# Experts of a group beside the two halves of the first attention of the next two groups

## The reference

```python
x = x + tanh(g_xattn[0]) * L0_xattn(layernorm(x), ctx)   # 16 heads of 16; q and k normed per head; the last
                                                         # 16 context rows have weights and a softmax of their own
x = x + tanh(g_ffn[0]) * L0_ffn(layernorm(x))            # router: top 4 of 16 experts of 64, and a shared expert
x = x + tanh(g_xattn[1]) * L1_xattn(layernorm(x), ctx)   # 16 query heads of 128, 8 key and value heads
x = x + tanh(g_ffn[1]) * L1_ffn(layernorm(x))            # weights looked up in a table of 16 values
```

## Time and profile before

| what | value |
|---|---|
| median of 3 runs | 504.74 us (504.55 to 507.48) |
| the profiled execution: own time | 506.47 us |
| the profiled execution: span | 504.5 us |
| mean granted TensorE clock, share of full | 0.904 |
| start to the first scores' end | 0 to 40.8 us |
| phase A from there | 40.8 to 163.1 us |
| phase B | 163.1 to 278.8 us |
| phases C and D | 278.8 to 504.5 us |

### The profile page before, as it was taken

One profiled execution on the slowest core, in us unless ns is written; L12 is line 12 of the kernel. 1 busy time (PEld: TensorE's weight loads), 2 busy tenths in 40 slices (PEclk: granted clock), 3 DMA queues, 4 the chain that ended last, 5 costly groups with the idle time before them and its releaser, 6 DMA issues.

```text
span 504.5 us, 8784 instructions
## 1 busy us (share of the span) xinstructions
PE 420.9 (83%) x3040; PEld 394.6 (78%) x3040; DVE 344.3 (68%) x754; ACT 204.9 (41%) x404; POOL 162.3 (32%) x195
## 2 busy tenths in 40 slices
PE   0546895958565999999999899999999999598896
PEld 0435774848465999999998899989988989597795
DVE  4776758486702657667675589889889979935542
ACT  2344535554311232333233366366366365222231
POOL 3014223131320121222313244463463564422232
PEclk9959695976855899999999999999999999988999
DMA  8102010010200002020200100100100100000000
GB/s 253 32 29 98 0 59 3 1 64 0 105 0 1 0 1 105 0 104 0 104 0 14 52 1 2 56 0 0 54 0 0 44 1 0 1 0 22 23 11 32
DMA packets 6633, 16.03 MB, mean 32 GB/s; under 512 B 1090, under 2 KB 4291, under 8 KB 6100
## 3 DMA queue, kind: packets, MB, share of 16 engines
q1 hardware_dynamic: 6612, 15.75, 9.3%
HBM read 14.70 MB, written 1.05 MB: 31 GB/s over the span
## 4 chain that ended last, share of the span: by engine, by line
PE 36%; issue 27%; DVE 15%; POOL 12%; ACT 7%; DMA 2%; POOLq 0%; DVEq 0%; ACTq 0%; SPq 0%
PE ps L290 19%; PE ps L485 5%; DVE work L1361 5%; POOL workr L1012 4%; PE ps L1091 4%; PE ps L475 2%; POOL workA L566 2%; ACT workA L510 1%; POOL wB_lo L572 1%; POOL rstd L255 1%; POOL work L1409 1%; POOL work L1419 1%; PE ps L360 1%; DVE shared_r L1323 1%; PE ps L1112 1%
## 5 line engine op out<-in xcount | busy, mean ns | idle before, releaser
L290 PE MATMUL ps<-wB_hi,workr 128*128 128x256 f32 (+1 forms) x224 | 52.7, 298 | 11.0 <-POOL workr L1574 10.2
L1419 POOL TENSOR_SCALAR work<-work,lut_step,lut 128x344 f32<-128x344 int32 (+1 forms) x60 | 41.7, 707 | 55.6 <-DVE work L1346 53.8
L290 PE MATMUL ps<-xT_hi,wB_hi 128*128 128x256 f32 x176 | 53.4, 303 | 0.0
L290 PE MATMUL ps<-xT_lo,wB_hi 128*128 128x256 f32 x176 | 51.6, 293 | 0.0
L290 PE MATMUL ps<-xT_hi,wB_lo 128*128 128x256 f32 x176 | 51.6, 293 | 0.0
L290 PEld LDWEIGHTS ps<-wB_hi,workr 128*128 128x128 f32 (+1 forms) x224 | 39.2, 192 | 13.2 <-issue 11.5
L290 PE MATMUL ps<-wN_hi,shared_r 128*128 128x256 f32 x256 | 48.0, 282 | 1.3 <-DVE x L1333 1.3
L1012 POOL TENSOR_TENSOR workr<-work,workr 128x256 fp32r<-128x256 f32 (+1 forms) x36 | 22.9, 637 | 74.1 <-ACT workr L895 74.1
L1361 DVE COPY_PREDICATED work<-work 128x1376 f32<-128x1376 int32 (+5 forms) x36 | 42.8, 1190 | 2.7 <-DVE work L1361 0.3
L290 PEld LDWEIGHTS ps<-wN_hi,shared_r 128*128 128x128 f32 x256 | 40.4, 188 | 1.5 <-DVE shared_r L1323 1.5
L290 PE MATMUL ps<-xT_hi,wM_hi 128*128 128x256 f32 x128 | 36.7, 287 | 3.9 <-ACT work L1187 2.4
(11 more groups left out here) (202 smaller groups left out, 1216.8 us busy)
## 6 DMA issues: line engine op xcount, KB each, us to landing
stage<-in_wC SPq DMA_DIRECT2D x4, 1280.0 KB, 5.4
stage<-in_wB SPq DMA_DIRECT2D x4, 768.0 KB, 4.3
stage<-in_idx SPq DMA_DIRECT2D x4, 536.0 KB, 3.4
stage<-in_wA SPq DMA_DIRECT2D x2, 512.0 KB, 5.5
out<-x SPq DMA_DIRECT2D x4, 256.0 KB, 2.2
x<-in_x SPq DMA_DIRECT2D x1, 768.0 KB, 7.1
ctx_T<-in_ctx_T SPq DMA_DIRECT2D x1, 512.0 KB, 7.4
ctx_n<-in_ctx_n SPq DMA_DIRECT2D x4, 128.0 KB, 2.2
```

Of the source, the lines that this page charges most:

```text
L290: last = nc.tensor.matmul(out, l, r, start=start and i == 0, stop=stop and i == 2)
L1419: nc.gpsimd.tensor_scalar(lev[:, j, 0:n], bits[:, 0, 0:n], lut_step[:, j:j + 1], lut[:, 2 * j:2 * j + 1], ALU.mult, ALU.add).then_inc(*C[" ...
```

## The change

Phases A and B become one. The new `pe_AB`, `act_AB`, `dve_AB` and `pool_AB` take four arguments: the group g, and whether the call does the experts of g, the second half of the attention of n = g+1, and the first half of the attention of m = g+2. The calls are `(-1, False, True, True)`, then a loop with `(g, True, True, True)` for g = 0 and 1, then `(2, True, True, False)` and `(3, True, False, False)`. Before them the first half of group 0 runs alone (`pe_A_first`).

With it come these changes:

- The gate banks are two instead of three and the spread bank is one. The logits share the spread's bank.
- A spread is one matmul: the upper and lower parts of the routing weights lie in one operand, at partitions 0 and 32.
- The layer norm's application in A and B moves from DVE to ACT (`front_norm_act`); it needs `rstd` and an `offset` from POOL (`front_pool_offset`).
- All eight slices of `kx` are made by ACT (`act_A_k`).
- All sixteen joins are done in the call for g = 3, two in each step; the weights for them come through two buffers.
- The expert weights are loaded at the start by four transfers, into the space of `wB_lo`, and split in the call for g = -1.
- The down products of all nine k use 128 rows (k = 8 used 64), and `rows_D` is 128 for all six.
- `pool_D` takes the lower parts of k = 0 and 1 before the front of the next group.

The core of the diff:

```diff
+        def front_pool_offset(pool, f):
+            front_pool(pool, f)
+            pool.wait_ge(*front["rstd_ready"].at(f, 1))
+            pool.sem_inc(waited, 1)
+            for t in range(TILES):
+                nc.gpsimd.tensor_scalar(offset[:, t:t + 1], mv[:, t, 0:1], rstd[:, t:t + 1], -1.0, ALU.mult,
+                                        ALU.mult).then_inc(*front["offset_ready"].up())
...
+        def front_norm_act(act, f, g):
+            act.wait_ge(*front["offset_ready"].at(f, TILES))
...
+            for t in range(TILES):
+                nc.scalar.activation(xn[:, t, :], x[:, g * TILES + t, :], ACT.Identity, scale=rstd[:, t:t + 1],
+                                     bias=offset[:, t:t + 1]).then_inc(*front["xn_ready"].up())
...
+        def act_A_k(act, n):
+
+            act.wait_ge(*A["qT_done"].at(n, 2))
+            for p in range(PAIRS0):
+                for i, (lo, hi) in enumerate(PARTS):
...
+        def pe_B_gate_up(pe, g, k):
+            pe.wait_ge(*Bp["h2"].at(g, k - 1))
...
+        def pe_B_spread(pe, g, k):
+
+            if k == 0:
...
+            else:
+                pe.wait_ge(*Bp["h3"].at(g, k))
+            nc.tensor.matmul(spread_to, sel[:, k, :], comb_rows, start=True, stop=True).then_inc(*Bp["bc_done"].up())
...
+        def pe_AB(pe, g, experts, second, first):
...
+            if experts:
+                pe_B_logits(pe, g)
+            if second:
+                pe_A_shift(pe, n, 0)
+                pe_A_shift(pe, n, 1)
+            if experts:
+                pe_B_gate_up(pe, g, 0)
+                pe_B_gate_up(pe, g, 1)
+                if last:
+                    pe_join(pe, 0)
+                    pe_join(pe, 1)
+                pe_B_comb(pe, g)
+                pe_B_gate_up(pe, g, 2)
...
+                pe_B_spread(pe, g, 0)
+            if second:
+                pe_A_probs(pe, n, 0)
+            if experts:
+                pe_B_gate_up(pe, g, 3)
...
+            if second:
+                pe_A_probs(pe, n, 1)
+            if experts:
+                pe_B_spread(pe, g, 1)
+                pe_B_down(pe, g, 0)
+            if first:
+                pe.wait_ge(*A["pT_ready"].at(n, 2))
+                front_pe(pe, front_A(m), A_FRONT)
+                pe_A_kv(pe, m, 0)
+            if experts:
+                pe_B_gate_up(pe, g, 4)
...
+                pe_B_spread(pe, g, 2)
+                pe_B_down(pe, g, 1)
+            if second:
+                pe_A_values(pe, n, 0)
+                pe_A_values(pe, n, 1)
+            if first:
+                x_split(pe, front_A(m))
+                pe_A_kv(pe, m, 1)
+            if experts:
+                pe_B_gate_up(pe, g, 5)
...
+            if second:
+                pe_A_turn_out(pe, n)
+            if first:
+                pe_A_q(pe)
+            if experts:
+                pe_B_gate_up(pe, g, 6)
...
+                pe_B_down(pe, g, 3)
...
+            if second:
+                pe_A_out(pe, n)
+            if experts:
+                pe_B_gate_up(pe, g, 7)
...
+                pe_B_down(pe, g, 4)
+            if first:
+                pe_A_turn(pe, m)
+            if experts:
+                pe_B_gate_up(pe, g, 8)
...
+                pe_B_spread(pe, g, 6)
+                pe_B_down(pe, g, 5)
+                pe_B_spread(pe, g, 7)
+            if first:
+                pe_A_scores(pe, m, 0)
+            if experts:
+                pe_B_down(pe, g, 6)
+                pe_B_spread(pe, g, 8)
+            if first:
+                pe.wait_ge(*A["o_biased"].at(n, 1))
+                pe_A_scores(pe, m, 1)
+            if experts:
+                pe_B_down(pe, g, 7)
+            front_pe(pe, front_next(g), B_FRONT)
+            if experts:
+                pe_B_down(pe, g, 8)
```

```diff
-        def rows_D(k):
-            return P if k < FC - 1 else FLAST
+            return P
...
         def pool_D(pool, g, more):
-            if more:
-                front_pool(pool, 13 + g)
             for k in range(FC):
+                if more and k == 2:
+                    front_pool(pool, 13 + g)
```

More of the change, by code:

```diff
@@ new lines, in joined, with join_bank, rows_B, gate_B @@
+        def joined(j, part):
+            first = j // 4 * HG + 2 * (j % 2)
+            return JOIN[j % 4][part][:, first:first + 2, :]
+        def join_bank(j):
+            return 4 + j % 4
+        def rows_B(k):
+            return P if k < EC else F
+        def gate_B(k):
+            return ps[:, k % 2, 0:TG]
+        def up_B(k):
+            return ps[:, k % 2, TG:2 * TG] if k < EC else gate_B(k)[F:2 * F]
+        def front_B(g):
+            return 7 if isinstance(g, int) and g == GROUPS - 1 else 2 * g + 2
@@ new lines, in pe_B_down @@
+        def pe_B_down(pe, g, k):
+            if k == 0:
+                pe.wait_ge(*Bp["x_done"].at(g, 0))
+            pe.wait_ge(*Bp["h_hi"].at(g, k + 1))
+            pe.wait_ge(*Bp["h_lo"].at(g, k + 1))
+            d_hi, d_lo = (ed_hi[:, k // 2, k % 2, :], ed_lo[:, k // 2, k % 2, :]) if k < EC else (sd_hi, sd_lo)
+            for t in range(TILES):
+                o, rows = ps[:, 3, t * D:(t + 1) * D], slice(t * P, (t + 1) * P)
+                nc.tensor.matmul(o, h_hi[k % 3][:, rows], d_hi, start=k == 0 and t == 0, stop=False,
+                                 skip_group_check=True)
+                nc.tensor.matmul(o, h_hi[k % 3][:, rows], d_lo, start=False, stop=False, skip_group_check=True)
+                last = nc.tensor.matmul(o, h_lo[k % 3][:, rows], d_hi, start=False, stop=k == EC,
+                                        skip_group_check=True)
+            if k == EC:
+                last.then_inc(*Bp["out_done"].up())
@@ new lines, in pool_AB @@
+        def pool_AB(pool, g, experts, second, first):
+            n, m = g + 1, g + 2
+            if second:
+                pool_A_scale(pool, n, 0)
+                pool_A_scale(pool, n, 1)
+            if first:
+                front_pool_offset(pool, front_A(m))
+            for k in range(6):
+                if experts:
+                    pool_B_lower(pool, g, k)
+                elif k < GROUPS:
+                    pool_A_prep(pool, k)
+            front_pool_offset(pool, front_next(g))
+            for k in range(6, EC + 1):
+                if experts:
+                    pool_B_lower(pool, g, k)
@@ L1722, in _ @@
                 pool_D(pool, g, g + 1 < GROUPS)
-        for name, phase, times in (("A", A, 3), ("B", Bp, 1), ("C", C, 2), ("D", Dp, GROUPS)):
+        for name, phase, times in (("A", A, 3), ("B", Bp, 3), ("C", C, 2), ("D", Dp, GROUPS)):
             for key, s in phase.items():
```

1045 lines of the change are left out of this document (542 added, 503 removed).

## The result

The changed kernel takes 544.58 us (median of 4 runs, 543.55 to 546.06), the kernel before 504.64: a ratio of 1.078, 95% interval 1.073 to 1.083. That is slower, as forecast, but 27 us above the predicted 517.3 and 12.6 above the upper end of the range. The profiled execution took 545.46 us, with a span of 543.3 and a mean clock of 0.877 where it had been 0.904.

What follows compares the result with a forecast made beforehand. A is bound by a chain through DVE, ACT and POOL, B by PE. 41 + 48 + 122 + 41.6 + 46.5 = 299.1 until C (+20.3), D and products -7.7: 504.7 + 12.6 = 517.3 us, range 485 to 532.

Steps and rivals of the forecast that it cites:

- Step 6: Full call, T+35.9 to T+45.0, from q to the scaled heads: 9.1 us, PE idle for 3.1.
- The edit in D: Phase D: two lower parts no longer stand behind rstd, so idles shrink and a clock fall goes: together -7.3 us.
- the short products' 0.4: Products of 128 rows instead of 48 or 64 cost the same and save switches: taken at -0.4 us.
- The 48 of call -1: Call -1, second half of group 0 and first half of group 1, no experts to fill it: 48 us.
- step 8: Full call, T+53.9 to T+58.2: spread, scores, down, spread, scores; the clock's fall adds 1.8 us.
- step 5: Full call, T+22.6 to T+35.9: PE's own work without a wait, from the front to q, 13.3 us.
- steps 2 and 3: Full call, T+5.1 to T+18.4: DVE's queue alone, then ACT's tanh(2) behind the norm; PE idles 2.2 and 2.4 us.
- step 3: Full call, T+14.8 to T+18.4: ACT's tanh(2) stands behind the norm and POOL; PE waits 2.4 us.
- step 7: Full call, T+45.0 to T+53.9: eight key slices and the norm precede tanh(8) on ACT; PE idles 5.7 us.
- (c): Rival: idles of 1.8 to 3 us keep the clock at half; a call takes 68 us, total 533; chance 0.12.
- steps 1 to 5: Full call, T to T+35.9: from the previous call's scores to q, at full clock.
- (a): Rival: helpers run ahead, hand-overs overlap more; change wins from calls of 54.6 us down; total 487 us; chance 0.19.

Runs made afterwards that it cites:

- three fills: Changed kernel with unread matmuls in three PE waits of calls 0 and 1 (ahead of spread(7), the turn and the front): 539.43 us, ratio 1.066.
- one fill: Changed kernel with 36 unread matmuls of 256 columns ahead of spread(7) in calls 0 and 1: 538.24 us, ratio 1.065.
- keys shared: Changed kernel with six key slices on DVE and two on ACT, instead of eight on ACT: 539.91 us, ratio 1.069.
- ACT's order alone: Changed kernel with ACT's queue reordered: tanh and upper steps ahead of norms, tanh(8) ahead of the key slices; no work added or moved elsewhere: 530.1 us, ratio 1.047.
- the mended kernel: Changed kernel with norm on DVE, key slices half and half on ACT and DVE, tanh(8) ahead of ACT's slices, fills of 12, 24 and 24: 513.33 us.
- the best fused one: The mended kernel with POOL's last lower part late, ACT's norm kept in call -1, fills of 48 and 24 there: 506.55 us, ratio 1.001.

## Why the prediction was wrong in size

**What held.** The sign, and the places of the waits. The longest wait of a full call is at spread(7) for weighted(6), 5.8 us (forecast 5.7); the turn waits 3.4 (3.1), `front_pe(m)` 2.1 (2.4). Step 6, from q to the scaled heads, took 9.2 (9.1); the key slices are 8 in 4.10 (3.65). The guess's table loads last 1.28 us, and Exp starts 0.02 behind the second, so the 4 to 8 us of draining that the prediction had worked out from the Trainium skill (ScalarE: Activation LUTs, What ACT_TABLE_LOAD costs) did not appear. The edit in D gave 7.7 in this kernel (7.3) and 5.8 in the one before; the short products' 0.4 can't be told from nothing. The start came 1.6 late and call -1 1.3. The 48 of call -1 is partly luck: no step had DVE's stand of 3.1 us beside POOL, and without it the call took 46.5.

**Where the time is.** C begins 25.0 us late: 1.6 in the start, 1.3 in call -1, 6.8 and 4.6 in the full calls, 5.3 and 5.5 in calls 2 and 3. Behind C's start, 6.5 us were won of the 7.7 forecast.

**The step that failed: the clock on top of a full call.** I added 3 us to 58.2 (1.8 in step 8; 0.9 and 0.3 for two idles that "drop it half the time"). Call 0's own rows give 6.4 over the full-clock steps: logits and their shifts 0.9, step 5 2.8 (16.1 instead of 13.3), and step 8, with spreads and downs slow beside the scores, 2.7 (7.0 instead of 4.3). So the clock was short by 3.4 of the 6.8 us of call 0. Two of the three parts were tested: three fills took step 5 back to 13.6, and one fill took step 8 back to 4.7. The idle of 2.13 us ahead of `front_pe(m)` had been given 0.9 us, as a fall that comes half the time; it cost 2.8, since behind it came 6 us of matmuls without a pause.

Calls 2 and 3, where 1.0 and 0.4 us were taken for the clock, have the same fault in part. No run put fills there, but runs with the very same instructions had another clock. First call 2 of the changed kernel and of "keys shared", then call 3 of the changed kernel and of "one fill":

```profile
225.26:272.17 46.91, 37.64 (x257) 35.67 (x256) 22.80 (x62) 14.62 (x33) 11.07 (x16) 0.83 0.08 29
```

```profile
221.54:266.63 45.09, 35.50 (x258) 33.46 (x256) 22.72 (x62) 14.68 (x33) 11.06 (x16) 0.89 0.08 30
```

```profile
272.17:324.14 51.97, 43.17 (x281) 40.94 (x280) 28.11 (x74) 17.45 (x41) 6.95 (x12) 0.80 0.18 64
```

```profile
266.44:316.32 49.88, 40.91 (x282) 38.75 (x280) 28.06 (x74) 17.45 (x41) 6.92 (x12) 0.86 0.19 67
```

So some 2 us of each are the clock at least. In call 3 they lie at its start, where PE works without a wait (the first 12.8 us at 0.69 and at 0.87), and not behind spread(7): that stretch takes 11.1 us in both, and 11.1 again in the run with the norm on DVE, where its mean clock is 0.63 instead of 0.50. In call 2, spread(7) started 38.5 us behind the logits where the sum had 34.8, though the clock was at full level from gate_up(2) to the end of down(5); which of its terms was short there stays open. ACT's order alone, without a fill, brought calls 2 and 3 to 41.9 and 49.4.

**Sizes of the steps.** The other 3.1 us or so of call 0: the small operations on the routing weights took 1.09 and 0.57 beside POOL's scaling, 0.17 and 0.19 without it (1.3 in all); the pair of norms on ACT took 1.09, twice, where I took 0.7 by the tanh's row (0.8); the slices 0.45. The rest is about what I lost in adding up: the parts named in steps 2 and 3 come to 10.0 and 3.8 us, and I wrote 9.7 and 3.6. (Step 5's parts come to 13.5, not 13.3, and PE's own 18.5 for the attention to 18.2.)

**The chain was right but not fixed.** In step 3 and step 7 I walked ACT's queue as written and got its price right. The run with another order shows what that price was: 14.5 us of the 40 lost, with what the clock adds behind these waits. The prediction had most of it in its sum, so it is a cause of the slowdown and not of the miss. The rest of the loss is the clock, the norm's and the slices' cost, and the filling and draining of the pipeline: calls -1, 2 and 3 took 148 us in the changed kernel and 136 in the best fused one, and only two of five calls overlap three parts.

**The rivals.** (c), the clock stays down, gave call 0 by its number (68; measured 67.8), missed call 1 by 2.4 and calls 2 and 3 by more. Its mechanism is half right: it let all of steps 1 to 5 stretch, and the windows of call 0 stand at 1.00 from 100 to 110 and from 120 to 140 us. What the Trainium skill says of such loops (TensorE: Matmul & The Clock Gate, HAM oscillation), that they can be throttled anew in every round, these windows bear out: the clock falls and comes back within the call. I held (c) at 0.12 because the trace before had one idle of each kind. (a), helpers that run ahead, was wrong for this order of the queues; in the mended kernel calls of 56 us come near its break-even of 54.6, with fills in them.

## What to carry to other kernels

When stages of several items are interleaved in one loop, walk every engine's queue at the steps where PE waits and move the short instruction that another engine needs ahead of the long one: here the order of one queue was worth 14.5 us. In the full calls here, PE's idles of 2.1 to 5.8 us were followed by half clock: price the whole burst behind such an idle, not the next instruction, and where nothing useful fits into it, try matmuls into a free bank, enough of them to leave little idle (1.4 us was little enough in one place) and not so many that they hold up what they wait for. Try them in the kernel before as well: there they gave 10 us, and that kernel is what the fused form has to be measured against. With four items and three overlapping parts, count the calls that are full before the overlap's gain is multiplied.

## What the runs showed of the hardware

- Useless matmuls made a kernel faster: 206 of them added 12 us of busy time to PE (415.4 to 427.5) and took 10 us off the total, with the mean clock going from 0.913 to 0.966.
- An idle of 1.39 us kept the clock up and one of 2.39 us at the same place did not (scores of 1.95 and 3.22 us). Idles between these two went either way: behind 1.89 us ahead of gate_up(2) the next 3 us ran at 1.00 in call 0 of the changed kernel, and behind 1.91 us at the same place at 0.52 in "keys shared".
- In three places a DVE copy or tensor_scalar that started while a POOL tensor_tensor on SBUF was running ended only with it: 3.97 instead of 0.87 us for two copies (the second alone 3.53), 3.75 instead of 0.73 for two norms, 1.09 instead of 0.17 for an operation on two columns. The first of the two copies, which started 0.05 us ahead of POOL's instruction, took its usual 0.41.
- An ACT activation of 128x256 from SBUF with a scale and a bias per partition took 0.59 us, where the tanh of the same shape from PSUM took 0.38.
